# Products that nobody reads on TensorE in the expert stage, and the recurrence's token loads issued by SyncE in place of GpSimd

## What is computed

```python
x = conv_recurrence(x)                       # 32 steps, two directions, sigmoid gates, residual
t = to_tokens(x)                             # [16, 1024, 64]
# selective state space, 128 channels x 128 states, 1024 steps:
xs, z = split(layernorm(t) @ W_in)
deltaA = exp((xs @ W_delta)[:, :, :, None] * A); deltaB = (xs @ W_delta)[..., None] * (xs @ W_B)[..., None, :]
state = deltaA * state + deltaB * x_i        # per step
y = (state . C_i) * silu(z); t = t + y @ W_out
# experts: each of 32 experts takes its 8 best tokens of 1024, pools them, runs a two-layer net, and
# adds the result back at these tokens
probs = softmax over tokens(layernorm(t) @ gate_w + gate_b); vals, idx = top_k(probs, 8)
pooled = sum_k vals * token[idx]; out = gelu([pooled, 1] @ weight1), then [.., 1] @ weight2
t = t + scatter_add(out * vals at idx)
```

## Time and profile before

| | |
|---|---|
| time, median of 3 runs | 6798.32 us (6797.84 to 6801.33) |
| the profiled execution: its time | 6799.73 us |
| its span, first to last instruction | 6797.9 us |
| mean granted TensorE clock | 0.978 |
| busy in the span: PE, DVE, ACT, POOL | 92%, 91%, 67%, 50% |
| busy in the scan stage (1950 to 6500 us): PE, DVE | 4206.86 and 4473.09 us of 4550 |

### The profile page before, as it was taken

One profiled execution on the slowest core, in us unless ns is written; L12 is line 12 of the kernel. 1 busy time (PEld: TensorE's weight loads), 2 busy tenths in 40 slices (PEclk: granted clock), 3 DMA queues, 4 the chain that ended last, 5 costly groups with the idle time before them and its releaser, 6 DMA issues. The chain is left out here.

```text
span 6797.9 us, 155743 instructions
## 1 busy us (share of the span) xinstructions
PE 6284.4 (92%) x52177; PEld 4061.5 (60%) x52177; DVE 6201.9 (91%) x3824; ACT 4529.4 (67%) x9559; POOL 3389.3 (50%) x8888
## 2 busy tenths in 40 slices
PE   8999989999969999999999999999999999999867
PEld 3678745466536666666666666666666666666535
DVE  7888878888849999999999999999999999999972
ACT  7888858888736666666666666666666666666641
POOL 5555545555445555555555555555455555554410
PEclk9999999999979999999999999999999999999995
DMA  6666666666622122121221212212122121221164
GB/s 143 153 156 154 155 144 155 153 156 153 152 68 57 43 57 48 44 59 42 55 51 42 59 47 51 50 42 61 45 51 51 41 62 45 51 49 42 26 187 114
DMA packets 831234, 563.52 MB, mean 83 GB/s; under 512 B 566029, under 2 KB 735917, under 8 KB 830637
## 3 DMA queue, kind: packets, MB, share of 16 engines
q1 hardware_dynamic: 765117, 522.72, 32.3%
q0 software_dynamic: 65536, 33.69, 2.2%
HBM read 159.23 MB, written 124.13 MB: 42 GB/s over the span
## 5 line engine op out<-in xcount | busy, mean ns | idle before, releaser
L1039 DVE TENSOR_TENSOR_SCAN states<-decay,enter_ps 128x1024 f32<-128x1024 f32 x2048 | 4468.6, 2262 | 88.7 <-PE enter_ps L727 61.7
L727 PEld LDWEIGHTS enter_ps<-s_steps,s_tokens 128*128 128x128 bf16 x16384 | 1597.1, 129 | 1421.5 <-DVE states L1039 1178.3
L852 ACT ACTIVATE decay<-rate_ps 128x512 f32<-128x512 f32 (+1 forms) x4096 | 2220.8, 594 | 329.5 <-PE rate_ps L713 141.8
L727 PE MATMUL enter_ps<-s_steps,s_tokens 128*128 128x128 bf16 x16384 | 2142.7, 310 | 298.5 <-DVE states L1039 294.0
L243 POOL TENSOR_TENSOR entered<-gates 128x512 f32<-128x512 f32 x512 | 900.2, 1758 | 889.1 <-ACT gates L203 889.1
L713 PE MATMUL rate_ps<-s_wide,s_decays 128*128 128x256 bf16 x8192 | 1319.9, 283 | 22.0 <-ACT decay L852 14.9
L952 POOL DMA_DIRECT2D s_tokens<-tokens_dram x2048 | 1047.2, 517 | 261.2 <-issue 218.7
L859 ACT COPY enter_ps<-at_first 128x16 f32<-128x16 f32 x1920 | 338.0, 176 | 1252.8 <-PE enter_ps L727 1165.4
L755 PE MATMUL y_ps<-states,spread 128*32 128x512 f32 x8192 | 1090.3, 604 | 2.4 <-issue 2.4
L971 POOL TENSOR_TENSOR product<-decay,states 128x16 f32<-128x16 f32 x1920 | 470.6, 245 | 1069.1 <-ACT decay L852 1053.4
L713 PEld LDWEIGHTS rate_ps<-s_wide,s_decays 128*128 128x128 bf16 x8192 | 902.1, 118 | 87.1 <-ACT decay L852 32.0
(11 more groups left out here) (136 smaller groups left out, 2635.4 us busy)
## 6 DMA issues: line engine op xcount, KB each, us to landing
rows<-feat SPq DMA_DIRECT2D x1024, 132.0 KB, 2.4
rows<-feat SPq DMA_DIRECT2D x512, 128.0 KB, 2.4
s_steps<-steps_dram SPq DMA_DIRECT2D x4096, 8.0 KB
rows<-feat SPq DMA_DIRECT2D x512, 127.8 KB, 2.4
s_wide<-rates_dram SPq DMA_DIRECT2D x1024, 32.0 KB, 1.8
s_tokens<-tokens_dram POOLq DMA_DIRECT2D x2048, 16.0 KB, 1.9
rates_dram<-parts SPq DMA_DIRECT2D x64, 384.0 KB, 3.3
steps_dram<-parts SPq DMA_DIRECT2D x64, 384.0 KB, 3.5
```

The costliest lines, as they stand in the source:

```text
L727: mm = pe.matmul(out.rearrange("p h l -> p l h"), tokens[s][:, k, :], steps[s][:, k, :, d:d + half], start=True, stop=True)
L852: act.activation(decay[i][:, half, at:], rate_ps[h][:, :, at:], ACT.Exp).then_inc(decay_ready, 1)
L1039: dve.tensor_tensor_scan(out, factor, term, 0.0, ALU.mult, ALU.add).then_inc(scanned, 1)
```

## The change

Two things change. The scan stage's token loads leave POOL's program and stand in SP's `load`, behind the sixteen loads of `steps`, and their semaphores start from the same offset as the others. In the expert stage PE runs f32 products of the identity with itself, 128 x 128 weights and 128 columns, into places of PSUM that nothing reads at that time: 60 behind the first `turn_tokens`, one behind the pooled sum of each batch (16), one behind each expert's first layer (32), and one behind every second expert's second layer (16).

```diff
-        tokens_in = [ctx.enter_context(nc.semaphore(f"scan_tokens_in{s}")) for s in range(SETS)]
+        tokens_in = [sem(f"tokens_in{s}") for s in range(SETS)]
@@ load(b, c) of SP, behind the loads of steps
+                for e in range(TERMS):
+                    a = STATE * (e // SPLITS)
+                    src = tokens_dram[bass.ds(b, 1), t0:t0 + SPAN, a:a + STATE].rearrange("b (k t) n -> (b t) k n", t=BLOCK)
+                    sp.dma_start(tokens[s][e::TERMS, :, :], src).then_inc(tokens_in[s], DMA)
@@ enters and first_steps of PE
-                    pe.wait_ge(tokens_in[s], (turn_of(b, c) + 1) * TERMS * DMA)
+                    pe.wait_ge(tokens_in[s], SCAN0 + (turn_of(b, c) + 1) * TERMS * DMA)
@@ POOL
-            def load_tokens(b, c, parts_of_eight):
-                s = set_of(c)
-                if c == 0:
-                    pool.wait_ge(parts_out[1], stores_to(b, len(STAGES) + 1))
-                pool.wait_ge(enter_ready, units_to(b, c - 1))
-                pool.sem_inc(passed, 1)
-                for e in parts_of_eight:
...
-                    if g in (1, 2, 3) and not (ending and c + 1 == CPB):
-                        load_tokens(*((b, c + 1) if c + 1 < CPB else (b + 1, 0)), range(3 * g - 3, min(3 * g, TERMS)))
...
-            load_tokens(0, 0, range(TERMS))
@@ PE of the expert stage
+            def idle_product(out):
+
+                pe.matmul(out, ident[:, :], ident[:, :], start=True, stop=True)
+
             turn_tokens(0)
+            for n in range(60):
+                idle_product(work_ps[:, 2, 0:128])
...
                     mm.then_inc(pooled_summed, 1)
+                    idle_product(work_ps[:, 2, 0:128])
...
                 if e % 16 == 15:
                     mm.then_inc(hidden_summed, 1)
+                idle_product(work_ps[:, 2, 0:128])
...
                 if e % 8 == 7:
                     mm.then_inc(results_summed, 1)
+                if e % 2:
+                    idle_product(chosen_ps[:, 0, :])
```

## The result

The changed kernel takes 6816.97 us (median of 11 runs, 6811.97 to 6820.21) against 6799.4 us for the kernel before, run beside it. The ratio is 1.0023, with a 95% interval from 1.0016 to 1.0031: it is slower, by about two parts in a thousand. The medians differ by 17.6 us. The profiled execution has a span of 6811.4 us and a time of 6813.24, one of the shortest of the eleven, and its span is 13.5 us longer than that of the kernel before; the other 4 us of the difference lie in no trace.

What follows compares the result with a forecast made beforehand. DVE was taken to bound the scan stage (4473.09 of 4550 us busy), half-clock PE the expert stage. From 6799.73, -13.3 (scan) and +28.2 (experts) gave 6814.6, as median 6813.2; range 6762 to 6820, the forecast's own 6808 to 6819.

Steps and rivals of the forecast that it cites:

- The pauses of POOL: Scan stage: 3.14 us pauses ahead of POOL's token loads would go with those loads, saving 16.3 us.
- the drifting gaps: Scan stage: 15 DVE waits for ACT, one in about 264 us, following POOL's pauses; together 16.3 us.
- SP's issues: Scan stage: eight more issues a chunk at 0.34 us, 2.7 us (bound 6.5), hidden except +3.0 us at the start.
- the thirty known gaps: Scan stage: DVE waits recurring with the batch, 0.18 and 0.43 us, 9.2 us in all, from ACT and PE; they stay.
- The block: Expert stage: 60 products raise the clock after at most 6 us, end about 6656.6, and cost nothing, being hidden.
- The gap behind it: Expert stage: PE, nearly idle between 6660 and 6665.2, is back at clock 0.50 when its unbroken chain begins.
- The small products' price: Expert stage at clock 0.50: 7.2 us in pooled sums, 13.3 in first layer, 7.7 in second; sum 28.2.
- The clock did come back inside the pooled sums: Rival, expert stage: full clock returns in the pooled sums and stays, 6765 us, chance 0.26; lost again, about 6795, 0.05.
- the clock did not come back in the second layer: Rival, expert stage: the clock comes back only in the second layer, 6798 us; chance 0.10.
- the pauses went with the loads: Rival, scan stage: pauses belong to POOL's program, not its loads, and stay; 6829 us, chance 0.03.
- SP was not late for DVE: Rival, scan stage: SP late with a chunk's operands from 5.2 us on, each microsecond costing 255 us; chance 0.02.
- The rule: Expert stage: the skill page gives unbroken work full clock; the trace had PE 37.95 of 40 us busy at 0.50.

Runs made afterwards that it cites:

- scan_only: Kernel before with only the token loads moved to SP, expert stage unchanged: 6784.28 us, ratio 0.9972.
- half_by_sp: Kernel before with every second token load on SP, the others still on POOL: 6790.28 us, ratio 0.9985.
- products_only: Kernel before with only the expert stage's added products, token loads still on POOL: 6833.33 us, ratio 1.0045.
- block_only: Kernel before with the block of 60 products alone, no single products: 6800.07 us, ratio 0.9997.
- gap_filled: Changed kernel with 18 more products behind batch 0's pooled sum and 8 behind the transposes of batch 2: 6813.53 us, ratio 1.0020.
- held_all: `held` with waits heading each four batches filled, 192-column products in the first layer, three products in the wait for the gelu: 6763.11 us, ratio 0.9944.
- second_block: Kernel before with token loads on SP and only a block of 16 products added, ahead of the second layer: 6779.86 us, ratio 0.9970.
- held: `gap_filled` with two products behind each pooled sum, one behind each expert of the first layer, none in the second: 6803.41 us, ratio 1.0004.
- no_block: Kernel before with the single products alone, without the block of 60, token loads on POOL: 6834.82 us, ratio 1.0048.
- held_first: `held_all` with the first chunk's eight token loads left to POOL: 6758.77 us, ratio 0.9944.

## Why the prediction was right

I forecast 6813 us from a profiled sum of +14.9 (-13.3 and +28.2). The profiled execution has +13.5, from -18.3 and +31.8, and the medians +17.6. The mechanisms of both halves were right, but each half was sized too small, by 5.0 and 3.6 us, and that these errors cancel is luck.

**The pauses of POOL** were the drifting gaps, shown by `scan_only` and by the count in `half_by_sp`. The size was too low. I took 16.3 us from the gaps as recorded; the recurrence, first scan to last, went from 4499.2 us (1974.21 to 6487.21 less 13.82) to 4477.45, 21.7 us less. Of these 0.7 is the second wait at the start, 1.3 us before and 0.6 after; it is 0.6 in `products_only` too, so the change did not bring it. The other 21.0 are the pauses. A gap costs some 0.3 us more than its own length (2.18 for 1.87). Part of it is that scans overlap by 0.1: one that stands alone takes 2.29 us in the record, while 81 in an unbroken row take 176.70, 2.18 each. The rest was not taken apart. At the end of the scans 17.2 us are left of this, behind a start that was 4.5 later, and the gate stage adds 1.1.

**SP's issues** are the step whose estimate was worst. I took 0.34 us each for their likeness to the `steps` loads and kept y's 0.82 as the bound; they measured 0.63. The page of before had the difference that I passed over: a load of tokens is 16 KB, one of `steps` 8. So the first scan came 5.0 us later behind the `steps` loads instead of 3.0. Further on DVE waits for nothing but the thirty known gaps, so the cost there was nothing, as said. But the room was not as I read it from one chunk. SP's own waits ahead of its loads of `wide` (L597) and `steps` (L604), two rows before and two after, say how much there was and how much is left:

```profile
SPq L597 <- PE rate_ps L713: 1312.5, 254, 9.5
SPq L604 <- PE enter_ps L727: 511.9, 254, 2.5
...
SPq L604 <- PE enter_ps L732: 238.8, 166, 2.5
SPq L597 <- PE rate_ps L718: 97.3, 73, 2.4
```

Before, SP waited at both places in all 254 chunks, 7.2 us a chunk; now it has 1.3 left. At L597 it comes too late to wait in 181 chunks, at L604 in 88, and still in time for DVE. I had said a few chunks and 0.8 us. Issues at my upper bound of 0.82 us each would have taken 1.5 us a chunk more than the measured ones, and by that estimate would have used the room up.

**The block** was hidden as said: `block_only` is at 0.9997. The gap behind it lost the clock as said: `gap_filled`, where it is filled, kept it there.

**The small products' price.** Pooled sums: 7.2 forecast, and from 6647.72 to 6704.85 it is 57.1 us against 49.8, +7.3. That agreement is partly luck: a batch took 3.61 us (pooled sums at 6647.72 and 6651.31), 0.72 more than 2.89 before, and the short return of the clock paid some of it back. First layer: 13.3 forecast, +13.1 measured (41.2 from 6704.85 to 6746.09, against 28.15 from 6715.04 to the second layer's start at 6743.19). Second layer: 7.7 forecast, +10.9 measured (38.5 us, against 27.6). That is the mis-sized term of this half: eight experts take 9.79 us, 2.91 more than 6.88, so a product costs 0.73 there and not 0.51. I had priced it by a row of like products back to back. Why one among others costs more was not taken apart.

**The rivals.** The clock did come back inside the pooled sums, for 3 us at 6694, and did not stay. As a description of this kernel that rival was wrong, but the stage can do what it said: in `held_all` it runs at 1.00 to the second layer's end. That its 6763 us is near the 6765 of my rival is in part luck, for the rival had no filled waits and put other sizes on the parts: 4, 5.7 and 9.9 us less for pooled sums, first and second layer, where `held_all` has 7.6, 2.6 and 10.3. My argument against the rival rested on rows at 0.50 with PE 95 and 98% busy. They show that such work doesn't raise the clock. They don't show that it can't keep it, and the second layer can: `second_block` has it at 1.00, unchanged. The other rivals fell: the clock did not come back in the second layer (0.50 from 6748 to 6785), the pauses went with the loads, and SP was not late for DVE.

**The rule.** The second layer was busy 27.00 of 27 us at 0.50 in one run and 17.00 of 17 at 1.00 in another, so being busy without a break did not bring the full clock here. The Trainium skill's page "TensorE: Matmul & The Clock Gate", section "Why this matters for your kernels", asks for unbroken work to reach the full clock, and these 27 us do not bear that out. It also says that idle gaps between bursts take the clock away. The changed kernel bears this out with its wait of 4.12 us; the clock was lost in `gap_filled` in shorter waits too, of 1.06 and 1.35 us close together. On transposes, the clock came back behind the eight 128-column transposes twice in `held`, and once each in the changed kernel, `products_only`, `no_block` and `held_first`. The same page's "Part 4: PE-mode transpose" lets one expect no help from them. But behind the other two such sets of the changed kernel (6657.36 and 6674.22), and behind both in the half-speed stretch of `gap_filled`, it did not come back, and no run took the transposes alone, so what they do stays open.

## What to carry to other kernels

Split a change whose parts touch different stages before judging it: this one held a gain of 19 us and a loss of 30. Work added to keep TensorE's clock paid here once it stood in the waits of the chain (`held_all`), and it belongs there first; single products between real ones, with the waits left open, cost their half-speed price and bought nothing. When the clock rises, the waits for the other engines grow, so look for them again in the new trace. An engine that carries a small step of a tight chain should not issue many small transfers beside it, and what counts is how many stand between two of its steps. A gap's price is read from the length of a whole row with it and without it. An issue on a queue is priced by its own pattern, and not by the nearest one's.

## What the runs showed of the hardware

- GpSimd paused some 3.2 us (2.95 where each load was split in two) after every 112 to 124 loads that it issued, of 16 KB or of 8; with 2048 loads of 16 KB that was once in 264 us.
- An issue on SyncE took 0.34 us for `steps` (8 KB each) and 0.63 for the tokens (16 KB); on GpSimd the tokens' took 0.52.
- Whether TensorE keeps 2.4 GHz and whether it gets it back are two questions: the second layer kept it unchanged (1.00 from 6736 to 6753 in `second_block`), and stayed at 0.50 for its whole 27 us when it began there (`scan_only`). Pooled sums and first layer, with products added, kept it in `held_all` (1.00 from 6650 to 6715).
- At twice the clock the second layer's small products ran 1.6 times as fast (0.86 against 0.54 us an expert), and the pooled sums with two added products 2.33 us a batch against 2.89 without any at half the clock.
